# Experts' weighted rows: accumulating indirect scatters into the output in place of a row table, eight gathers and a final sum

## What is computed

```python
x = hidden_states.reshape(-1, H)                     # 512 tokens, 128 features
probs = softmax(x @ gate_W)                          # 8 experts
rw, sel = jax.lax.top_k(probs, 2)                    # two experts for each token
rw = rw / rw.sum(axis=-1, keepdims=True)
w_full = jnp.sum(one_hot(sel, 8) * rw[..., None], axis=1)
...
expert_out = jnp.concatenate([mlp_out, kan_out], axis=0)   # (8, 512, 128)
out = jnp.einsum('eth,te->th', expert_out, w_full)
```

## Time and profile before

| | us |
|---|---|
| median of three runs | 193.28 |
| span of the profiled execution | 190.3 |
| PE busy (share of the span) | 129.7 (68%) |
| DVE busy | 121.2 (64%) |
| ACT busy | 64.5 (34%) |
| POOL busy | 45.9 (24%) |
| first rows of an expert (output 0) complete in `yn` | 153.16 |
| last rows (output 7) complete in `yn` | 176.64 |
| first gather starts | 176.28 |
| last gather has landed | 187.97 |

### The profile page before, as it was taken

One profiled execution on the slowest core, in us unless ns is written; L12 is line 12 of the kernel. 1 busy time (PEld: TensorE's weight loads), 2 busy tenths in 40 slices (PEclk: granted clock), 3 DMA queues, 4 the chain that ended last, 5 costly groups with the idle time before them and its releaser, 6 DMA issues.

```text
span 190.3 us, 3087 instructions
## 1 busy us (share of the span) xinstructions
PE 129.7 (68%) x974; PEld 112.9 (59%) x974; DVE 121.2 (64%) x319; ACT 64.5 (34%) x165; POOL 45.9 (24%) x65
## 2 busy tenths in 40 slices
PE   0570595879799945953014399999999999998000
PEld 0340573768699835732004389999879989897000
DVE  2578250588777670967898678779365589981121
ACT  2031024215157661621522044424008399610000
POOL 1758504017069300004184000000000000000771
PEclk9996589999999997999555559999999999999855
DMA  5999999000000000009920000000000010100222
GB/s 133 345 459 434 391 362 259 6 3 2 3 2 3 0 9 3 0 2 344 427 112 3 0 2 0 0 3 0 0 0 3 0 36 16 38 19 17 59 61 73
DMA packets 8658, 17.27 MB, mean 91 GB/s; under 512 B 1080, under 2 KB 7096, under 8 KB 7992
## 3 DMA queue, kind: packets, MB, share of 16 engines
q1 hardware_dynamic: 7800, 16.00, 22.6%
q0 software_dynamic: 256, 0.52, 1.0%
q10 hardware_dynamic: 576, 0.42, 0.7%
HBM read 14.06 MB, written 2.88 MB: 89 GB/s over the span
## 4 chain that ended last, share of the span: by engine, by line
PE 55%; DVE 20%; issue 9%; DMA 7%; POOL 4%; ACT 2%; POOLq 1%; SPq 1%; DVEq 0%; ACTq 0%
PE A L798 13%; PE A L938 10%; PE C L926 5%; PE D L994 5%; DMA arena<-mask 4%; PE C L814 4%; DVE arena L1468 3%; POOL arena L543 3%; PE A L973 2%; PE D L749 2%; DVE x L1296 2%; PE D L983 2%; DMA arena<-y_table,dest 1%; PE A L814 1%; PE A L953 1%
## 5 line engine op out<-in xcount | busy, mean ns | idle before, releaser
L798 PE MATMUL A<-arena 128*128 128x128 f32 x176 | 24.1, 294 | 12.3 <-DVEq L400 6.8
L798 PEld LDWEIGHTS A<-arena 128*128 128x128 f32 x176 | 22.1, 204 | 15.3 <-DVEq L400 7.6
L543 POOL DMA_INDIRECT arena<-y_table,dest x8 | 7.8, 980 | 75.7 <-issue 75.7
L1161 DVE TENSOR_TENSOR arena<-A,arena 128x1024 f32<-128x1024 f32 x11 | 13.5, 1224 | 18.4 <-PE A L798 18.4
L505 POOL TENSOR_TENSOR arena<-arena,mxb 128x512 f32<-128x512 f32 x14 | 14.1, 1040 | 26.0 <-issue 18.5
L938 PE MATMUL A<-arena,kw 128*128 128x161 f32 x128 | 18.9, 302 | 0.3 <-DVE arena L1417 0.3
L994 PE MATMUL D<-arena 128*128 128x161 f32 x128 | 18.8, 301 | 0.3 <-DVE arena L1468 0.3
L938 PEld LDWEIGHTS A<-arena,kw 128*128 128x128 f32 x128 | 17.9, 190 | 1.3 <-DVE arena L1417 0.7
L994 PEld LDWEIGHTS D<-arena 128*128 128x128 f32 x128 | 17.7, 189 | 0.9 <-issue 0.5
L613 ACT ACTIVATE arena<-C 128x512 f32<-128x512 f32 x16 | 8.8, 594 | 20.4 <-PE C L814 20.4
L604 ACT ACTIVATE arena<-arena 128x512 f32<-128x512 f32 x22 | 13.2, 630 | 6.9 <-DVE arena L1171 3.0
(11 more groups left out here) (187 smaller groups left out, 242.1 us busy)
## 6 DMA issues: line engine op xcount, KB each, us to landing
kw<-KW SPq DMA_DIRECT2D x1, 4096.0 KB, 17.3
arena<-KW SPq DMA_DIRECT2D x1, 4096.0 KB, 13.1
mw<-MW SPq DMA_DIRECT2D x2, 1024.0 KB, 20.1
y_table<-zeros SPq DMA_DIRECT2D x8, 240.0 KB, 6.1
arena<-ctxT SPq DMA_DIRECT2D x4, 256.0 KB, 8.9
arena<-mask SPq DMA_DIRECT2D x1, 1024.0 KB, 8.2
y_table<-arena SPq DMA_DIRECT2D x8, 64.0 KB, 1.6
cst<-consts SPq DMA_DIRECT2D x1, 256.5 KB, 8.8
```

The source lines that it names most:

```text
L543: pool.indirect_dma_start(out=yg[:, k, i], out_offset=None, in_=y_table if k else y_table[0:(EX - 1) * ROWS, :], in_offset=bass.IndirectOf ...
L798: last = mm(A[k % 2][:, h * P:(h + 1) * P], QM[:, b, h], kT[:, b, t * P:(t + 1) * P], start=True, stop=True)
L1161: v.tensor_tensor(s, A[k % 2][:, :].rearrange("p (h k) -> p h k", h=H), bias(mbias[:, b, t]), ALU.add).then_inc(scores_kept, 1)
```

## The change

The row table, its clearing, the stores into it, the eight gathers, the final sum on DVE and the four stores of the result go. In their place:

- `out` has 160 more rows after the 512 tokens', into which unused places are added. SP clears them, and stores `x2` into the 512 rows as soon as the last layer's normalisation has begun (after `xf_made` 1).
- A `slot_table` in HBM says, for each place of each expert, its token and its weight (8 bytes). SP first fills it with defaults (an unused row, weight 0). After `route_weights`, POOL writes the tokens' pairs into it by eight indirect scatters of 128 pairs. SP reads it back to `slot` (two DMAs, `slots_in`).
- `rows_out` multiplies by the place's weight as it copies, and so waits for `slots_in`.
- POOL adds each output's rows to `out` by two indirect scatters with add (128 rows, then 32). From output 1 on it first waits until both scatters of the output before have landed, since both experts of a token add into the same row.
- `dest_made` comes at the end of `route_weights`, and a small conversion is added there.
- In `layer1`, `to_rows` stands before `g = 2` and no longer before `g = 4`.

```diff
-            for e in range(EX):
-                sp.dma_start(y_table[e * ROWS + SLOTS:(e + 1) * ROWS, :].rearrange("(p r) w -> p r w", p=ZP),
-                             zeros[0:ZP, 0:P].unsqueeze(1).broadcast_to([ZP, (ROWS - SLOTS) // ZP, P])).then_inc(rows_cleared, 16)
+            sp.dma_start(out[B * P:B * P + P, :], zeros[:, 0:P]).then_inc(out_set, 16)
+            sp.dma_start(out[B * P + P:, :], zeros[0:REST, 0:P]).then_inc(out_set, 16)
...
+            sp.wait_ge(xf_made, 1)
+            sp.dma_start(out[0:B * P, :].rearrange("(b q) d -> q b d", b=B), x2[:]).then_inc(out_set, 16)
+
+            def slots_of(row):
+                for j, n in ((0, P), (1, REST)):
+                    sp.dma_start(slot[0:n, j].rearrange("p e w -> p (e w)"),
+                                 slot_table[bass.ds(row + j * P * EX, n * EX), :].rearrange("(p e) w -> p (e w)", e=EX)).then_inc(slots_in, 16)
+
+            sp.wait_ge(slots_put, 32 * B)
+            slots_of(0)
...
+            sp.wait_ge(out_set, 48)
+            sp.wait_ge(added, 32 * EX)
...
+            pool.wait_ge(slots_cleared, 16)
+            pool.wait_ge(dest_made, 1)
+            for k in range(2):
+                for i in range(B):
+                    pool.indirect_dma_start(out=slot_table, out_offset=bass.IndirectOffsetOnAxis(ap=dest[:, k, i:i + 1], axis=0),
+                                            in_=pair[:, k, i], in_offset=None).then_inc(slots_put, 16)
+
+            def add_rows(r):
+                pool.wait_ge(slots_in, r * 32 + 32)
+                for n in range(EX):
+                    pool.wait_ge(*rows_kept(r, n))
+                    if n:
+                        pool.wait_ge(added, r * (32 * EX) + 32 * n)
+                    pool.sem_inc(rows_due, 1)
+                    for j, m in ((0, P), (1, REST)):
+                        pool.indirect_dma_start(out=out, out_offset=bass.IndirectOffsetOnAxis(ap=slot[0:m, j, n, 0:1], axis=0),
+                                                in_=yn[0:m, n, j], in_offset=None, compute_op=ALU.add).then_inc(added, 16)
...
-            for k in range(2):
-                if k:
-                    pool.wait_ge(y_stored_last, 32)
...
-                for i in range(B):
-                    pool.indirect_dma_start(out=yg[:, k, i], out_offset=None,
-                                            in_=y_table if k else y_table[0:(EX - 1) * ROWS, :],
-                                            in_offset=bass.IndirectOffsetOnAxis(ap=dest[:, k, i:i + 1], axis=0)
-                                            ).then_inc(y_back[k][i], 16)
...
                 def layer1(n):
                     pe.wait_ge(yT_kept, r * EX + E2 + n - 1)
                     for g in range(G):
-                        if g == 4:
+                        if g == 2:
                             to_rows(E2 + n - 1)
...
                 def rows_out(n):
                     dve.wait_ge(yn_made, r * EX + n + 1)
-                    v.tensor_copy(yn[:, n, 0], YN[n % 2][:, 0:P])
-                    v.tensor_copy(yn[0:REST, n, 1], YN[n % 2][0:REST, P:2 * P]).then_inc(yn_kept_mlp, 1)
+                    dve.wait_ge(slots_in, r * 32 + 32)
+                    v.tensor_scalar(yn[:, n, 0], YN[n % 2][:, 0:P], weight[:, 0, n:n + 1], None, ALU.mult)
+                    v.tensor_scalar(yn[0:REST, n, 1], YN[n % 2][0:REST, P:2 * P], weight[0:REST, 1, n:n + 1], None, ALU.mult
+                                    ).then_inc(yn_kept_mlp, 1)
...
-            own_done()
-            for i in range(B):
-                dve.wait_ge(y_back[0][i], 16)
-                own(v.scalar_tensor_tensor(fin[:, i], yg[:, 0, i], wgt[:, 0, i:i + 1], x2[:, i], ALU.mult, ALU.add))
-            own_done()
-            for i in range(B):
-                dve.wait_ge(y_back[1][i], 16)
-                v.scalar_tensor_tensor(fin[:, i], yg[:, 1, i], wgt[:, 1, i:i + 1], fin[:, i], ALU.mult, ALU.add).then_inc(fin_made, 1)
```

More of the change, by code:

```diff
@@ L137, in layer @@
         dest = sb("dest", [P, 2, B], U32)
+        pair = sb("pair", [P, 2, B, 2], U32)
+        slot = sb("slot", [P, 2, EX, 2], U32)
         cmax = sb("cmax", [1, 1])
@@ L347, in layer @@
         yn_kept_kan = sem("yn_kept_kan")
-        y_stored = sem("y_stored")
-        y_stored_last = sem("y_stored_last")
         fv = sem("fv")
[L351 to L355, removed]
+        slots_cleared = sem("slots_cleared")
+        slots_put = sem("slots_put")
+        slots_in = sem("slots_in")
+        out_set = sem("out_set")
+        rows_due = sem("rows_due")
+        added = sem("added")
         FAR = float(1 << 20)
         def last_round_stored(eng, r):
-            eng.wait_ge(y_stored, r * STORED)
-            eng.wait_ge(y_stored_last, r * 32)
+            eng.wait_ge(added, r * (32 * EX))
         def tanh_bias(g):
@@ L453, in _ @@
                 with sp.Fori(1, ROUNDS) as r:
-                    store_round(r, r * SLOTS)
-            for i in range(B):
-                sp.wait_ge(fin_made, i + 1)
-                sp.dma_start(out[:, i], fin[:, i]).then_inc(out_done, 16)
-            sp.wait_ge(out_done, 16 * B)
+                    last_round_stored(sp, r)
+                    slots_of(r * (SLOTS * EX))
+                sp.wait_ge(added, ROUNDS * 32 * EX)
+            sp.wait_ge(out_set, 48)
+            sp.wait_ge(added, 32 * EX)
         @block.gpsimd
@@ L527, in _ @@
                 rstd_step(j)
+            pool.wait_ge(slots_cleared, 16)
[14 more added lines that the diff above has]
+                                                in_=yn[0:m, n, j], in_offset=None, compute_op=ALU.add).then_inc(added, 16)
+            pool.wait_ge(out_set, 48)
+            add_rows(0)
             pool.wait_ge(over_made, 1)
             over = pool.value_load(over_i[0:1, 0:1])
-            pool.wait_ge(rows_cleared, 16 * EX)
-            pool.wait_ge(y_stored, STORED)
             with pool.If(over > 0):
-                pool.wait_ge(y_stored, ROUNDS * STORED)
-            pool.wait_ge(dest_made, 1)
-            for k in range(2):
-                if k:
-                    pool.wait_ge(y_stored_last, 32)
-                    with pool.If(over > 0):
-                        pool.wait_ge(y_stored_last, ROUNDS * 32)
-                for i in range(B):
-                    pool.indirect_dma_start(out=yg[:, k, i], out_offset=None,
-                                            in_=y_table if k else y_table[0:(EX - 1) * ROWS, :],
-                                            in_offset=bass.IndirectOffsetOnAxis(ap=dest[:, k, i:i + 1], axis=0)
-                                            ).then_inc(y_back[k][i], 16)
+                with pool.Fori(1, ROUNDS) as r:
+                    last_round_stored(pool, r)
+                    add_rows(r)
         @block.scalar
@@ L1345, in _ @@
             own(v.scalar_tensor_tensor(posm[:], pos, 1.0, sel[:], ALU.add, ALU.mult))
-            own(v.tensor_tensor(rowid[:], pos, eoff.unsqueeze(1).broadcast_to([P, B, EX]), ALU.add))
+            own(v.scalar_tensor_tensor(rowid[:], pos, float(EX), eoff.unsqueeze(1).broadcast_to([P, B, EX]), ALU.mult, ALU.add))
             dve.wait_ge(dv, count[0] - 1)
@@ L1362, in route_weights @@
                 own(v.tensor_scalar(dest[:, 0], destf[:, 0], FAR, None, ALU.add))
-                v.tensor_copy(dest[:, 1], destf[:, 1]).then_inc(dest_made, 1)
+                own(v.tensor_copy(dest[:, 1], destf[:, 1]))
+                own(v.tensor_copy(pair[:, :, :, 0], token_no.unsqueeze(1).broadcast_to([P, 2, B])))
                 own(v.tensor_tensor(mask_k[:, 1], dtmp[:, 1], destf[:, 1].unsqueeze(2).broadcast_to([P, B, EX]), ALU.is_equal))
@@ L1375, in route_weights @@
                 own_done()
-                own(v.tensor_tensor(wgt[:], wsum[:], wden[:].unsqueeze(1).broadcast_to([P, 2, B]), ALU.mult))
+                v.tensor_tensor(pair_w, wsum[:], wden[:].unsqueeze(1).broadcast_to([P, 2, B]), ALU.mult).then_inc(dest_made, 1)
             def ffn(r, again, off):
@@ L1603, in build @@
         args.append(nc.dram_tensor(name, value.shape, mybir.dt.from_np(value.dtype), kind="ExternalInput").ap())
-    out = nc.dram_tensor("out", (B, P, P), F32, kind="ExternalOutput").ap()
+    out = nc.dram_tensor("out", (B * P + SLOTS, P), F32, kind="ExternalOutput").ap()
     args[2] = args[2].bitcast(U8) if args[2].dtype != U8 else args[2]
-    layer(nc, *args, out.rearrange("b q d -> q b d"))
+    layer(nc, *args, out)
 def kernel(**inputs):
@@ L1616 @@
     r = run_bass_kernel_spmd(nc, [arrays], core_ids=[0])
-    return r.results[0]["out"]
+    return r.results[0]["out"][0:B * P].reshape(B, P, P)
```

35 lines of the change are left out of this document (14 added, 21 removed).

## The result

The changed kernel takes 206.57 us (median of four runs, 204.69 to 208.47) against 194.04 us before on the same chip, a ratio of 1.068 (95% interval 1.062 to 1.074). It is 6.8% slower. The forecast was 191.3 us, a little faster than before, in a range from 185.5 to 199. Medians are those of all runs of a kernel, while ratios compare only its fast executions, so that the two can differ by some tenths of a per cent.

The account below looks back on a forecast made before the run. Until the last expert PE sets the pace, then a tail of POOL issue, landing and store; the change makes a chain of eight scatter steps. Start 153.46 plus 8 x 4.35 gives span 188.36, time 191.3 us, range 185.5 to 199.

Parts of the forecast that it names:

- P: Period of one scatter step in the tail, from one pair to the next: 4.35 us, taken eight times, ends 3.2 and 6.3.
- term (1): POOL's issue of the 128-row scatter and the gap after it, taken as for the gathers: 0.94 and 0.30 us.
- DVE in POOL's way: Rival, slower: nine issues up to 171 us each wait for one DVE instruction of 0.41, adding 3.7 us, 195.0; chance 0.06.
- What bounds it: PE sets the pace to the last expert, then POOL's issue, one landing and one store; afterwards the scatter chain sets the end.
- The start: POOL's first scatter into the output: rows ready at 153.16, plus 0.30, so first issue at 153.46 us.
- (4): Correction for the second issue having 32 rows, not 128: saves between nothing and 0.70 us, taken as 0.20.
- term (5): Correction for the add's output read and HBM write, within the transfer: between 0 and 1.5 us, taken as 0.36.
- Dear adds: Rival, slower: accumulation costs most of a store on top in each step, period 5.3, span 195.96, time 198.9 us; chance 0.22.
- The cheap steps: Rival, faster: short issue for 32 rows and the add hidden, period 3.6, span 182.36, time 185.3 us; chance 0.36.
- The moved transposes: In layer1(1), PE waits about 1.4 us for DVE; output 7 comes 1.1 us later, at 177.7, hidden by the chain.
- Routing: Slot table written after route_weights and read back by 136 us at most, needed at 152.68: 16 us of cover.
- The start of the kernel: The eight clearing stores hold SP from 7.14 to 30.98 us; removing them gains nothing.

Follow-up runs that it names:

- e11: The changed kernel once more, unaltered: 205.27 us against 194.18 before, ratio 1.067 (1.058 to 1.076).
- e7: The changed kernel with POOL's first scatter into the output held until the rows of all eight outputs are complete: 225.86 us, a single execution.
- e6: The changed kernel with one operand of DVE's squares read from PSUM (results wrong): 201.83 us, ratio to before 1.045 (1.036 to 1.055).
- e1: The changed kernel with the add taken out of the scatters into the output (sum over experts missing): 193.54 us, ratio to before 1.000.
- e3: The kernel before with only the transposes moved, to before g = 2 from g = 4: 194.5 us, ratio 1.002 (0.995 to 1.008).
- e8: The changed kernel with the transposes back before g = 4: 203.94 us, ratio to before 1.061 (1.052 to 1.070).
- e4: The changed kernel with the eight clearing stores put back at the start: 204.58 us, ratio to before 1.065 (1.050 to 1.079).
- e5: The changed kernel with plain scatters into two planes, no add or waits between pairs, DVE summing, transposes at g = 4: 190.53 us, ratio to before 0.990.
- e2: The changed kernel with a separate target tensor per expert and no waits between pairs (sum over experts missing): 190.45 us, ratio to before 0.987.

## Why the prediction was wrong, step by step

The step that failed is the period P of the chain, and in it term (1), the issue on POOL "as the gathers have it": 0.94 us was taken, and an issue with the add measured 1.55. A second cost, DVE's squares in POOL's way, was right as a mechanism, but was left out of the sum and given a chance of 0.06. Together they turn the forecast's small gain into the measured loss of 6.8%.

**What bounds it** was right: the tail was one chain on POOL, and the change put eight steps in its place, each released by a landing. Step 7 begins 17.6 us after its rows in the first profile (6 forecast).

**The start** was right in e11: 153.61, forecast 153.46. That is luck in part: POOL took 0.90 us from the rows (152.38 + 0.33) and not 0.30, but the rows were complete 0.45 us sooner in that execution.

**P** failed, 5.41 and not 4.35. By its terms, against e7:

| | forecast | measured |
|---|---|---|
| issue of 128 rows | 0.94 | 1.55 |
| gap | 0.30 | 0.30 |
| issue of 32 rows | 0.94 - 0.20 = 0.74 | 1.33 |
| end of issue to the next pair | 2.65 - 0.94 + 0.36 + 0.30 = 2.37 | 2.21 (mean of 7) |
| sum | 4.35 | 5.39 |

(With the first pair, which is slightly longer, the mean of the seven periods is 5.41.) The failed terms are (1), "as the gathers have it", and with it (4). A gather and a plain scatter cost the same on POOL (0.94 and 0.97), but an accumulating one costs 0.6 more, and 32 rows save next to nothing (0.11 plain, 0.22 with the add). I had looked for the add's price in the landing, term (5), where only 0.2 to 0.3 of it are. The landing with its 0.36 for the add and the 0.30 for the resume were together 0.16 too much. The error of 1.04 us went in eight times: 8.3 us, which alone makes 191.3 to 199.6.

**DVE in POOL's way** was put aside with 0.06, though the issues did become 3.1 to 4.1 us longer beside DVE (3.7 forecast). That the size agrees is luck. The forecast's sum was 0.41 us, one DVE instruction, at each of nine issues. What happened is narrower: one or two issues are held until the end of a whole group of squares, and the operand change in e6 takes that away. The Trainium skill, "SBUF — State Buffer", section "Who interferes with whom", says that a DVE instruction with two SBUF inputs contends with GpSimd's reads. e6 agrees with this, 4.11 us against 1.56. The same section of the Trainium skill adds that a probe didn't see `tensor_tensor` stall DMAs issued from GpSimd, and infers a reason. Here issues of indirect DMAs were held beside it (4.11 to 4.36 us in four profiles).

**The rivals added up.** Dear adds (P = 5.3, 198.9 us) had the right size for P. Adding 3.7 to 5.2 us for the overlap gives 202.6 to 204.1, and 0.11 x 8 for the rest of P brings it to 203.5 to 205.0, against 205.27 in e11 and 206.57 with the late start. (These sums go from span to time by the forecast's 3.0 us. The profiled executions of the changed kernel took 1.8 us more than their span, 206.94 against 205.1, so that up to 1.2 us of the agreement is loose.) I treated the two as alternatives. They act on the same chain, one on every step and one on some, so the range should have reached to their sum. It ended at 199.

**The cheap steps** had 0.36, and no run supports them. Even without the add a step took 4.06 us (e1), where they needed 3.6. The estimate P = 3.6 rested on the Trainium skill, "DMA: Bandwidth & Descriptors", section "Anatomy of one DMA — SWDGE (gpsimd) path", which gives about 2.0 us for one DMA. With 0.30 for the resume that is 2.3 us from the start of the second issue to the next pair. Measured are 1.33 + 2.21 = 3.54 us, and 0.86 + 1.93 = 2.79 without the add, so these DMAs take longer than the page gives.

**The moved transposes** were right in mechanism and size: PE waited 1.71 us (1.60 in e3; 1.4 forecast), output 7 came 1.1 us later (e8), and the chain covered it. **The scaling** in `rows_out` was put at nothing and isn't quite: its copies take 0.35 and 0.33 us where they took 0.29 and 0.27. That is under cover too. **Routing** was right: SP reads the slots at 137.02 in the first profile, 19 us before the first row copy at 156.09, and at 133.15 in e11. **The start of the kernel** was right: with or without the clearing stores (e4, e11) the kernel's time is the same within its intervals.

## What to carry to other kernels

Before several results are added by DMA into one place, multiply the whole step (issue, second issue, landing, resume) by the number of steps that must wait for each other, and compare with the tail it replaces: 8 x 5.4 = 43 us could not fit into the 37 us between the first rows, 153.2, and the old end, 190.3. Where each value has a known number of summands, give each summand its own place and add on an engine. The scatters then wait for nothing but their rows, and a slow issue is hidden. Here that was worth 1% (e5), with an interval that reaches from 2% to almost nothing. When two rivals act on one chain, the range must hold their sum.

## What the runs showed of the hardware

- An accumulating indirect DMA occupies POOL 1.55 us for 128 rows of 512 bytes and 1.33 us for 32 (e7), a plain one 0.97 and 0.86 (e1). A quarter of the rows saves only a seventh or a ninth of the issue.
- From the end of the issue to POOL's next DMA behind the landing: 2.1 to 2.4 us undisturbed with the add (e7), 1.93 without (e1). Beside the experts' work it reached 3.48 (e11).
- Several accumulating scatters in flight to different tensors do not lengthen each other's issue (e2).
- Issues beside DVE products with both operands in SBUF took up to 4.36 us (e8), but not every one (1.66 in the changed kernel). With one operand in PSUM they took 1.33 to 1.61 (e6).
- A held issue with the add of 128 rows ended 1.44 or 1.45 us after DVE's group, whenever it had begun (four profiles).
